# In an attention stage that shares seven PSUM banks as a ring, a pair of banks that would wrap round the ring's end is placed ahead of the score pair instead

## The reference: a feed-forward mixture, attention, and the mixture again

```
x = x + 0.5 * ffn(layernorm(x), ...)     # 8 experts, each token goes to its best 2
x = x + attn(layernorm(x), W_qkv, W_o)   # 16 heads of 8 features
x = x + 0.5 * ffn(layernorm(x), ...)
```

```
qkv = (x @ W_qkv.T).reshape(b, n, H, DH).transpose(0, 2, 1, 3)      # q = k = v
score = jax.nn.softmax(jnp.einsum('bhif,bhjf->bhij', qkv, qkv) / SQRT_D, axis=-1)
attn = jnp.einsum('bhij,bhjf->bihf', score, qkv)
out = attn.reshape(b, n, F) @ W_o.T
```

## Time and profile before

| | |
|---|---|
| median of 3 runs | 1383.12 us (1382.29 to 1386.11) |
| profiled execution, span from first to last instruction | 1384.9 us |
| PE (TensorE matmul) busy over the span | 1247.0 us, 90% |
| DVE (VectorE) busy | 1168.4 us, 84% |
| ACT (ScalarE) busy | 894.7 us, 65% |
| POOL (GpSimd) busy | 540.0 us, 39% |
| L1969, one reduction of 1024 values, x443 | 534.1 us, mean 1222 ns |
| L1487, one exponential of a bank, x1024 | 556.3 us, mean 596 ns |

### The profile page before, as it was taken

One profiled execution on the slowest core, in us unless ns is written; L12 is line 12 of the kernel. 1 busy time (PEld: TensorE's weight loads), 2 busy tenths in 40 slices (PEclk: granted clock), 3 DMA queues, 4 the chain that ended last, 5 costly groups with the idle time before them and its releaser, 6 DMA issues.

```text
span 1384.9 us, 29603 instructions
## 1 busy us (share of the span) xinstructions
PE 1247.0 (90%) x10053; PEld 645.8 (47%) x10053; DVE 1168.4 (84%) x2335; ACT 894.7 (65%) x1881; POOL 540.0 (39%) x665
## 2 busy tenths in 40 slices
PE   3738999787699999999999999999999989899993
PEld 3736888776123222322323323233322237778882
DVE  8877888787998898889898888988899648888886
ACT  1214555555188888888778787788877875455652
POOL 3873557243543002234234424323442215653332
PEclk9999999999599999999999999999999999999997
DMA  8115655553211210112011021011100222555663
GB/s 269 41 68 186 208 197 182 216 196 104 73 42 53 73 27 13 36 37 72 19 43 50 15 59 37 18 34 55 36 4 18 90 97 97 190 175 196 240 217 132
DMA packets 65383, 135.58 MB, mean 98 GB/s; under 512 B 13330, under 2 KB 34932, under 8 KB 65204
## 3 DMA queue, kind: packets, MB, share of 16 engines
q1 hardware_dynamic: 56052, 115.39, 24.7%
q0 software_dynamic: 8704, 16.93, 3.8%
q10 hardware_dynamic: 480, 1.38, 0.3%
HBM read 47.35 MB, written 25.07 MB: 52 GB/s over the span
## 4 chain that ended last, share of the span: by engine, by line
PE 54%; DVE 25%; issue 6%; POOL 5%; ACT 4%; DMA 3%; SPq 1%; DVEq 0%; ACTq 0%; POOLq 0%
PE psum L2283 13%; DVE att_neg_part L1969 12%; PE psum L2259 8%; PE psum L2193 6%; PE psum L2181 6%; PE psum L2183 6%; PE psum L2263 5%; PE psum L2240 5%; POOL rows_dram L1295 4%; DMA ffn_block_rows<-rows_dram 2%; DVE att_neg_part L1974 2%; DVE ffn_x2c L1910 2%; DVE stats L1608 1%; DVE ffn_hidden L1921 1%; ACT att_probs L1487 1%
## 5 line engine op out<-in xcount | busy, mean ns | idle before, releaser
L1487 ACT ACTIVATE att_probs<-psum 128x512 f32<-128x512 f32 x1024 | 556.3, 596 | 121.3 <-PE psum L2265 89.0
L1969 DVE TENSOR_REDUCE att_neg_part<-psum 128x2 f32<-128x1024 f32 x443 | 534.1, 1222 | 58.4 <-PE psum L2241 45.5
L2283 PE MATMUL psum<-att_probs,att_values 128*16 128x256 f32 x4096 | 320.3, 385 | 6.1 <-ACT att_o_t L1502 3.7
L1454 ACT ACTIVATE ffn_silu<-ffn_x2c,ffn_rec 128x256 f32<-128x256 f32 (+1 forms) x320 | 154.8, 487 | 172.2 <-DVE ffn_x2c L1910 129.8
L1311 POOL DMA_INDIRECT y_dram<-ffn_y,ffn_block_rows x144 | 143.2, 995 | 238.1 <-ACT ffn_y L1472 202.4
L2240 PE MATMUL psum<-att_right,att_left 64*128 64x512 bf16 x512 | 197.7, 387 | 13.4 <-DVE att_neg_part L1969 8.9
L2259 PE MATMUL psum<-att_right,att_left 64*128 64x512 bf16 x512 | 198.8, 388 | 5.1 <-DVE att_neg_part L1969 4.6
L2262 PE MATMUL psum<-att_right,att_left 64*128 64x512 bf16 x512 | 198.8, 388 | 3.7 <-DVE att_neg_part L1969 1.9
L1910 DVE TENSOR_SCALAR ffn_x2c<-psum,ffn_rec 128x256 f32<-128x256 f32 (+1 forms) x320 | 162.6, 512 | 44.1 <-PE psum L2183 37.5
L2241 PE MATMUL psum<-att_right,att_left 64*128 64x512 bf16 x512 | 198.2, 388 | 0.0
L2263 PE MATMUL psum<-att_right,att_left 64*128 64x512 bf16 x512 | 193.8, 379 | 0.0
(11 more groups left out here) (222 smaller groups left out, 1540.2 us busy)
## 6 DMA issues: line engine op xcount, KB each, us to landing
ffn_rec<-record SPq DMA_DIRECT2D x80, 776.5 KB, 3.8
ffn_block_rows<-rows_dram SPq DMA_DIRECT2D x64, 130.0 KB
att_left<-q_parts_dram SPq DMA_DIRECT2D x64, 96.0 KB
att_right<-q_parts_dram SPq DMA_DIRECT2D x124, 48.0 KB
record<-in_L_ffn_W SPq DMA_DIRECT2D x16, 256.0 KB, 6.5
att_right<-q_parts_dram SPq DMA_DIRECT2D x92, 32.0 KB
y_dram<-ffn_y,ffn_block_rows POOLq DMA_INDIRECT x144
q_parts_dram<-att_parts SPq DMA_DIRECT2D x12, 192.0 KB
```

What stands on the lines that cost most here:

```text
L1487: S.activation(probs[:, slot % PROBS, :], ring_bank(("score", slot))[:, :], ACT.Exp, scale=SCALE).then_inc(att_bank.by_act, 1)
L1969: last = V.tensor_reduce(out=neg_part[:, h % 2, keys, p::PAIR, t], in_=psum[:, low:high + 1, :], axis=AX.X, op=ALU.max, negate=True)
L2283: last = TE.matmul(value_bank[head * VS:head * VS + VW, q], values[:, b % 2, kt, team * TEAM + head, :], probs[:, (UNIT * n + j) % PROBS, ...
```

## The change

Three things change. `Ring.plan` leaves the last bank empty (a holder `None`) where a max unit would start in it, so that the unit takes banks 0 and 1, and `empty_before` steps over such an empty place to the holder before it. The planner of the attention tests before each score pair whether the max unit behind it would start in the last bank, which is so when the next bank is 4; in that case it plans the max unit first (banks 4 and 5) and the score pair behind it (banks 6 and 0), and `tensor_attention` fills them in that order. In `vector_row_max` the case with two reductions goes.

```diff
--- before.py
+++ after.py
@@ -63,11 +63,16 @@
 
     def plan(self, name, size=1):
         assert name not in self.at, name
+        if size == 2 and self.next_bank() == self.banks - 1:
+            self.holders.append(None)
         self.at[name] = len(self.holders)
         self.holders += [name] * size
         self.count[size] += 1
         self.number[name] = (size, self.count[size])
 
+    def next_bank(self):
+        return len(self.holders) % self.banks
+
     def bank(self, name, k=0):
         return (self.at[name] + k) % self.banks
 
@@ -81,8 +86,13 @@
 
     def empty_before(self, name):
 
-        first = self.at[name] - self.banks
-        earlier = {self.holders[k] for k in range(first, first + self.number[name][0]) if k >= 0}
+        earlier = set()
+        for k in range(self.at[name], self.at[name] + self.number[name][0]):
+            k -= self.banks
+            while k >= 0 and self.holders[k] is None:
+                k -= self.banks
+            if k >= 0:
+                earlier.add(self.holders[k])
         return [self.emptied(other) for other in sorted(earlier, key=lambda other: self.at[other])]
 
 
@@ -748,11 +758,17 @@
             if n == HALF_UNITS + 1:
                 for chore in first_chores:
                     plan_banks(*chore)
+        max_ahead = set()
         for slot in range(0, NSCORES, 2):
+            if (att_bank.next_bank() + 2) % att_bank.banks == att_bank.banks - 1:
+                max_ahead.add(slot)
+                for n in max_units(slot + 1):
+                    att_bank.plan(("max", n), 2)
             att_bank.plan(("score", slot))
             att_bank.plan(("score", slot + 1))
-            for n in max_units(slot + 1):
-                att_bank.plan(("max", n), 2)
+            if slot not in max_ahead:
+                for n in max_units(slot + 1):
+                    att_bank.plan(("max", n), 2)
             for chore in chores[slot] + chores[slot + 1]:
                 plan_banks(*chore)
         for slot in HEAD + TAIL:
@@ -1965,15 +1981,8 @@
             h = 2 * i + g
             V.wait_ge(maxed, n + 1)
             low, high = max_banks(n)
-            if high == low + 1:
-                last = V.tensor_reduce(out=neg_part[:, h % 2, keys, p::PAIR, t], in_=psum[:, low:high + 1, :],
-                                       axis=AX.X, op=ALU.max, negate=True)
-            else:
-
-                for k, where in enumerate((low, high)):
-                    last = V.tensor_reduce(out=neg_part[:, h % 2, keys, PAIR * k + p, t:t + 1], in_=bank[where],
-                                           axis=AX.X, op=ALU.max, negate=True)
-            last.then_inc(reduced, 1)
+            V.tensor_reduce(out=neg_part[:, h % 2, keys, p::PAIR, t], in_=psum[:, low:high + 1, :],
+                            axis=AX.X, op=ALU.max, negate=True).then_inc(reduced, 1)
             if n % HALF_UNITS == HALF_UNITS - 1:
                 V.wait_ge(reduced, n + 1)
                 if h >= 2:
@@ -2214,9 +2223,13 @@
                     for chore in first_chores:
                         tensor_chore(*chore)
             for slot in range(0, NSCORES, 2):
+                if slot in max_ahead:
+                    for n in max_units(slot + 1):
+                        tensor_row_max(n)
                 tensor_scores(slot)
-                for n in max_units(slot + 1):
-                    tensor_row_max(n)
+                if slot not in max_ahead:
+                    for n in max_units(slot + 1):
+                        tensor_row_max(n)
                 if slot >= UNIT:
                     tensor_values(slot // UNIT - 1, slot % UNIT // 2)
                 for chore in chores[slot] + chores[slot + 1]:
```

## The result

Timed beside the kernel before, the change took 1405.4 us (median of four runs) against 1385.03 (median of five). The measured ratio is 1.0145, with a 95% interval from 1.0131 to 1.0159. A second comparison on another chip gave 1.0144 (1.0126 to 1.0161), with 1399.38 against 1378.92 us. The chips differ more in level (0.4% between these two, for the same kernel) than the two ratios do, so I compare ratios, and turn them into us at 1385: the change costs 20 us. The forecast was +16 (1399, range 1386 to 1411).

A forecast was written before the change was run, and what follows sets the result against it. It took TensorE to be the bound, held up now and then by VectorE. The terms 0.2 + 4.9 + 12 - 1 = +16 us gave a forecast of 1399 us, range 1386 to 1411.

The forecast's parts named there:

- Bound and mechanism: Attention: TensorE bounds at 1.31 us a block; the unit behind a moved max unit waits for that one's reduction.
- Ordinary places: Moved max units whose reduction isn't late: 18 lose 0.2 us in all, 22 lose 4.9 in all, 0.22 each.
- tight places: Max units that must wait for the reduction of the unit just before: 8 before the change, 72 after.
- Late places: 24 moved max units that VectorE comes to late: 12 us, 0.5 each, bounds 5 and 21.7.
- The reductions: VectorE's row maximum, 69 pairs of reductions become 69 single ones: -1 us, bounds 0 and -4.1.
- ScalarE and the empty places: Moved blocks' scores reach ScalarE 0.22 us later; 7 empty ring places among the first 26 units: both costed at nothing.
- the idle time before L2253's matmuls: Sign: TensorE's wait for reductions ahead of the max unit, longer by some 15 us, at up to 46 places.
- the block behind an ordinary moved one: Sign: TensorE's pitch 0.2 us longer in the block behind a moved max unit, 1.31 elsewhere.
- the attention's stretch: Sign: the attention about 16 us longer, the stages ahead of it and behind unchanged.
- The waits ahead of L2275: Sign: this line waits for reductions less often than 52 times.
- The reading that VectorE holds TensorE up for 18.6 us: Kernel before: TensorE's waits ahead of L2262, weight loads included, 18.6 us in 52 waits.

The follow-up runs named there:

- a_pairs: The change's order and ring, but each of the 65 moved max units reduced by two instructions of 512 values; 1.0163 of the kernel before.
- s_best: Against the kernel before: max unit planned between its two scores, only in blocks where no chore takes a bank, 53 reduction pairs gone; 1.0003.
- a_short: The change with reductions of only the first 256 of each bank's 512 scores; 0.9836 of the kernel before.
- b_short: The kernel before with reductions of only the first 256 of each bank's 512 scores; 0.9808 of the kernel before.
- m_free: The kernel before, ring and reduction pairs kept, with the max unit filled ahead of the score pair in 65 blocks; 1.0025 of the kernel before.

## Why the prediction held, term by term

- **Bound and mechanism.** TensorE's 1.31 us per block and the distance of one unit between a filling and the reduction it waits for were right: 20.9 us hang on that one wait.
- **Ordinary places, 0.2 + 4.9 us.** Measured 7.8 with the pairs of reductions. Less their share, about half of the 2.7 us by which a_pairs is slower, that is some 6.4. One number was off. I took 0.06 us from a reduction's end to the matmul that waits, as read at L2262. At the max unit it is 439.22 - 439.07 = 0.15. Of the 72 tight places 57 bind, that is, their max unit starts within 0.17 us of the reduction's end, and of these 49 take 0.15 and 8 take 0.06. So the ordinary place costs 0.3 us in place of 0.21.
- **Late places, 12 us of at most 21.7.** Measured 12.9 with the pairs, less the other half some 11.5. What they would lose alone was right: in the trace after, their max units came 22.7 us late in all against before. The part that is given back, 3.8 us in the next blocks and 7.3 elsewhere, I had estimated at 10, by choice of 0.5 us a place rather than by a sum. That the term came out so close is in part luck.
- **The reductions, -1 us.** In the change's order single reductions are worth 2.7 us (a_pairs), since the next unit waits for a moved unit's end. That is the pairs' share taken off the two terms above, which were worked out with single ones. Beside it, in an order without further tight places, 53 single ones are worth nothing that shows (s_best), where I had taken 1 us.
- **ScalarE and the empty places, 0 us.** The moved blocks kept 1.31 us. The 3.9 us between a_short and b_short are the most that order, ring and the tight waits still binding cost there.

The measured terms sum to 20.9 - 2.7 = 18 us for the change, which took 20. The intervals are 1.3 to 2.4 us wide to each side, so nothing is left that I could name. The forecast's 16 was 4 short, of which the ordinary places' hand-over makes 1.3 and the reductions 1. The late places took 0.5 less than forecast, and the remaining 2 us aren't assigned.

Of the signs named ahead, the idle time before L2253's matmuls grew by 20 us and not 15, the block behind an ordinary moved one by 0.3 and not 0.2, and the attention's stretch by 17.7 and not 16. The waits ahead of L2275 fell to 16 as they should. The reading that VectorE holds TensorE up for 18.6 us was too small, as b_short shows; no term of the sum rests on it.

## What to carry to other kernels

A ring of buffers is not only so many slots. Each slot's last user decides whom the next one waits for, and a reordering that removes a wrap can put a unit right behind its own predecessor. List for every filling how many units back its release lies, before and after, and price each place at which that falls to one: the consumer's duration and two hand-overs, less the time until the filling is due. Two reductions in place of one cost VectorE 0.06 us here, and the kernel nothing that can be measured while the distance is kept; a lost unit of distance cost TensorE 0.3 us at an ordinary place and 1.3 at the late one shown, part of which came back.

## What the runs showed of the hardware

- How soon a matmul starts after its release depends on how the wait stands in TensorE's list. A max unit that has two fillings to wait for has a separate wait instruction ahead of its weight load in the trace. (The views above leave such instructions out.) One that has a single filling to wait for has the wait on the weight load itself, as L2262 has. Of the 57 max units held until the reduction before theirs ends, the 49 with the separate instruction start 0.145 to 0.147 us after its recorded end, and the 8 without it 0.056 to 0.058, as does L2262 in the kernel before. ScalarE as the releaser gives the same 0.144 to 0.145 us, at 33 moved units of m_free, all with the separate instruction. The weight loads of unit 72, whose reduction before ends at 439.07, and of unit 114, where it ends at 498.08 + 2.35 = 500.43:

```profile
439.19 0.09 PEld L2253 LDWEIGHTS psum<-att_right,att_left 64*128 64x128 bf16 x1 [0.61 <-DVE att_neg_part L1984]
```
```profile
498.08 2.35 DVE L1984 TENSOR_REDUCE att_neg_part<-psum 128x2 f32<-128x1024 f32 x2
```
```profile
500.48 0.09 PEld L2253 LDWEIGHTS psum<-att_right,att_left 64*128 64x128 bf16 x1 [0.69 <-DVE att_neg_part L1984]
```

- At 37 of these 49 units both waits are for reductions, as at unit 72 (`reduced 71` and `reduced 72`), and the lower count is implied by the higher. To leave it out would save 0.09 us at each by these rows, an estimate of some 3 us at most. No run tries it.
- Two PSUM reductions of 512 values cost VectorE 0.06 us more than one of 1024 where they follow without a wait (1.19 against 1.13 us), though their recorded durations sum to 0.14 more.
- The kernel before took 1378.9, 1387.4 and 1385.6 us (medians) on the three chips of the experiments, so that a difference under 0.6% can be read only from runs on the same chip.
